# Conv 1: the scaling of the nodes' centred rows on ScalarE in eight pieces in place of one VectorE operation

## The reference, cut to what matters

```python
h = jnp.maximum(_layernorm(x, axis=-1), 0.0)
x = x + _L0_gnn_ref(h, edge_index, edge_attr_2, W1, root1, bias1, W2, root2, bias2)
# in it, twice (spline_conv):
xk = jnp.einsum('ni,kio->nko', x, W)              # 25 matrices of 64x64
msg = msg + basis[:, None] * xk[src, idx]         # four corners of the edge's cell
agg = jax.ops.segment_max(msg, dst, num_segments=N)
return agg + x @ root + bias                      # nodes without an edge: 0 + x @ root + bias
# the norm:
(x - m) / jnp.sqrt(v + eps)                       # m and v over the 64 channels of a node
```

## Time and profile before

| | |
|---|---|
| median of 3 runs | 1747.36 us |
| profiled execution | 1748.64 us, its span 1746.8 us |
| mean granted TensorE clock | 0.955 of full speed |
| busy over the span: PE | 1471.2 us, 84% |
| DVE (VectorE) | 1395.1 us, 80% |
| POOL (GpSimd) | 1225.4 us, 70% |
| ACT (ScalarE) | 731.8 us, 42% |

### The profile page before, as it was taken

The page is one execution under the profiler, slowest core; times in us unless marked ns, Lnnn a source line. Parts: engine busy times, 40 slices in busy tenths (PEclk is TensorE's granted clock), DMA queues, the critical chain, the costliest instruction groups (busy, mean ns, idle before and its releaser), DMA issues.

```text
span 1746.8 us, 33764 instructions
## 1 busy us (share of the span) xinstructions
PE 1471.2 (84%) x7834; PEld 1002.3 (57%) x7834; DVE 1395.1 (80%) x2704; ACT 731.8 (42%) x1840; POOL 1225.4 (70%) x1207
## 2 busy tenths in 40 slices
PE   3978888888888879999999999997777777777673
PEld 2856666666666656777777777774444333333332
DVE  6259999999999957988888888885776666666664
ACT  3533333333333353333333333335554555555553
POOL 5027777777777757777777777743677777777776
PEclk8989999999999979999999999997998999998998
DMA  8994444444445435878787777863333233323330
GB/s 136 160 121 107 105 106 110 105 107 107 110 104 108 98 91 155 213 215 216 213 212 209 208 209 211 208 177 82 78 70 70 69 70 70 72 71 66 73 72 18
DMA packets 451934, 218.45 MB, mean 125 GB/s; under 512 B 306089, under 2 KB 432058, under 8 KB 451896
## 3 DMA queue, kind: packets, MB, share of 16 engines
q1 hardware_dynamic: 355584, 138.37, 31.1%
q0 software_dynamic: 44864, 65.52, 17.6%
q10 hardware_dynamic: 51448, 14.14, 6.4%
HBM read 128.08 MB, written 92.64 MB: 126 GB/s over the span
## 4 chain that ended last, share of the span: by engine, by line
PE 34%; POOL 9%; issue 8%; ACT 5%; DVE 4%; DMA 4%; POOLq 0%; DVEq 0%; ACTq 0%; SPq 0%
PE bank L1016 17%; POOL gath L610 5%; POOL out_dram L617 4%; PE bank L1009 3%; PE bank L1146 3%; DMA gath<-M,gidx 2%; PE bank L1077 2%; PE bank L1060 2%; PE bank L1165 1%; DVE arena L1636 1%; PE bank L1049 1%; PE bank L1038 1%; PE bank L1069 1%; DVE arena L1624 1%; ACT arena L915 1%
## 5 line engine op out<-in xcount | busy, mean ns | idle before, releaser
L1016 PE MATMUL bank<-Wk,arena 128*128 128x320 f32 (+1 forms) x2352 | 652.8, 460 | 56.9 <-ACT arena L786 56.9
L610 POOL DMA_INDIRECT gath<-T,gidx x392 | 397.6, 1014 | 121.5 <-issue 117.6
L1016 PEld LDWEIGHTS bank<-Wk,arena 128*128 128x128 f32 (+1 forms) x2352 | 328.2, 189 | 262.0 <-issue 145.5
L786 ACT ACTIVATE arena<-bank 128x256 f32<-128x256 f32 (+1 forms) x392 | 169.7, 433 | 349.7 <-PE bank L1009 349.6
L610 POOL DMA_INDIRECT gath<-in_x_dram,gidx x196 | 194.7, 993 | 141.8 <-ACT gidx L706 83.3
L610 POOL DMA_INDIRECT gath<-M,gidx x196 | 211.1, 1077 | 108.6 <-issue 54.5
L617 POOL DMA_INDIRECT T<-srow,sidx x196 | 206.7, 1055 | 69.6 <-issue 59.4
L617 POOL DMA_INDIRECT out_dram<-srow,sidx x196 | 199.7, 1019 | 61.4 <-issue 60.8
L1425 DVE TENSOR_TENSOR arena<-bank,A 128x320 f32<-128x320 f32 x392 | 190.9, 487 | 57.7 <-PE bank L1016 53.6
L1009 PE MATMUL bank<-ident,arena 128*128 128x128 f32 x980 | 171.7, 274 | 12.4 <-DVE arena L1405 12.4
L1009 PEld LDWEIGHTS bank<-ident,arena 128*128 128x128 f32 x980 | 124.1, 141 | 43.4 <-issue 12.6
(11 more groups left out here) (212 smaller groups left out, 2685.9 us busy)
## 6 DMA issues: line engine op xcount, KB each, us to landing
T<-arena SPq DMA_DIRECT2D x96, 272.0 KB, 3.9
arena<-T SPq DMA_DIRECT2D x48, 544.0 KB, 5.5
T<-zero ACTq DMA_DIRECT2D x1, 13281.2 KB, 100.9
B<-arena SPq DMA_DIRECT2D x49, 256.0 KB, 3.3
arena<-B SPq DMA_DIRECT2D x49, 256.0 KB, 3.7
arena<-in_x_dram SPq DMA_DIRECT2D x48, 256.0 KB, 4.0
out_dram<-arena SPq DMA_DIRECT2D x48, 256.0 KB
begins_cut<-begins_d SPq DMA_DIRECT2D x49, 128.5 KB, 3.4
```

What stands on the lines that cost most here:

```text
L610: pool.indirect_dma_start(out=gath[slot][:, j, k, 0:width], out_offset=None, in_=table, in_offset=bass.IndirectOffsetOnAxis(gidx[slot][:, ...
L786: act.activation(ZT[j // 2][:, first:first + chunks, :], bank[j % 2][:, 0:chunks * P], ACT.Relu)\
L1016: return pe.matmul(bank[2 + r][:, 0:KO], ZT[q][rows, chunk, :], Wk[n - 1][rows, weights].rearrange("p k o -> p (k o)"), start=start, stop= ...
```

## The change

ScalarE does what `node_in` did: eight `activation` instructions with function Copy, one for each of the eight node tiles, each with its reciprocal deviation (one value per partition, a column of `jst`) as scale. They stand in ScalarE's step behind the index copy `gidx1(g + 3)` and ahead of the two small copies; the last of them signals `xn`. `node_in` leaves VectorE's step. As ScalarE now reads the reciprocals, VectorE's `roots` waits for `xn` of group e - 2 before it writes new ones.

```diff
+                    if n == 1 and g.within(G):
+                        wait(act, s["norm"], g + 1, "rstd")
+                        wait(act, s["ncen"], g)
+                        wait(act, s["npe"], g - 1, "nt")
+                        for t in range(NPP):
+                            scaled = act.activation(nh[:, t, :], nln[:, t, :], ACT.Copy,
+                                                    scale=jst[:, 3, TPG + t:TPG + t + 1])
+                        scaled.then_inc(s["xn"].sem, 1)
...
-                def node_in(g):
-                    wait(dve, s["norm"], g + 1, "rstd")
-                    wait(dve, s["npe"], g - 1, "nt")
-                    V_.tensor_tensor(nh[:, :, :], nln[:, :, :],
-                                     jy[:, TPG:].unsqueeze(2).broadcast_to([P, NPP, C]), ALU.mult)\
-                        .then_inc(s["xn"].sem, 1)
...
                     def roots():
                         if stats:
                             wait(dve, s["root"], e)
+                            wait(dve, s["xn"], e - 2)
                             V_.reciprocal(jy, jt).then_inc(s["norm"].sem, 1)
 
-                    if now and n == 1:
-                        node_in(g)
                     if ahead and n == 1:
                         scaled(g + 1)
```

## The result

The changed kernel takes 1751.67 us, the median of 13 runs (1748.94 to 1754.53); the kernel before took 1747.36 on the same chip (13 runs, 1744.55 to 1750.21). The ratio is 1.0025 [1.0016, 1.0033]: slower by 0.25%, or 4.3 us. The forecast was 12.6 us slower. The profiled span grew from 1746.8 to 1751.8 us.

A forecast was written before the change was run, and what follows sets the result against it. GpSimd was to bound conv 1 once VectorE got faster: 43 groups at 10.98 us gave +14.5, less 0.4 and 1.2, so +12.9 on the profiled 1748.64, 1761.5; 1.3 lower for the median gave 1760 us, range 1737 to 1782.

The forecast's parts named there:

- GpSimd is at work all the time and becomes the bound: Conv 1: GpSimd works or issues throughout its 10.52 us group; once VectorE is faster, GpSimd sets the pace.
- Its stalls come from VectorE's operations on two SBUF inputs: Conv 1: GpSimd's DMAs are held beside such VectorE operations; stalls of 0.40 us a group before the change.
- ScalarE's copies cost nothing: Conv 1, ScalarE: eight copies, 1.6 to 3.0 us a group, hidden in 3.67 us idle before its evacuation.
- The size of the stalls when VectorE follows GpSimd: Conv 1, GpSimd: 0.86 us a group, near attention's 0.77 and a little up, giving 10.98 us a group.
- the sum's 12.9: Whole kernel: +14.5 us over 43 conv 1 groups, -0.4 for the margin, -1.2 in the last two groups.
- The floor of 10.12: Conv 1, GpSimd: a group of four undisturbed gathers and four undisturbed scatters with gaps takes 10.12 us.
- rival 3: Conv 1: GpSimd has no stalls, 1723 us, or is no limit at all, 1718 us; chance 0.07.
- VectorE alone could go at 9.92: Conv 1, VectorE: removing L1452's 0.60 us shortens its loop from 10.52 to 9.92 us a group.
- The margin at the end: End of conv 1: time from the fourth gather's start to VectorE's use falls from 3.34 to about 2.9 us.
- Rival 1: Conv 1: GpSimd's stalls fall to 0.2 us a group with a lucky landing, 10.32 us, 1737 us; chance 0.12.
- rival 2: Conv 1: the phase locks again with about today's 0.40 us of stalls a group, 1746 us; chance 0.10.
- Rival 4: Conv 1: a DMA lands before a 1.9 us row of VectorE operations each group, stalls 1.4, 1784 us; chance 0.15.

The follow-up runs named there:

- e4_after_light: The changed kernel with three scatters a group in conv 1 in place of four; 1742.06 us, 0.9947 of the kernel before.
- e10_one_input: The changed kernel with nine VectorE operations in a conv 1 group written as reductions reading one SBUF input; 1735.14 us, 0.9924 of the kernel before.
- e1_both: The changed kernel with a spare VectorE product on two SBUF inputs in the removed operation's place, copies kept; 1752.92 us, 1.0000 of the kernel before.
- e3_one_copy: The changed kernel with one unscaled ScalarE copy of 128x512 in place of the eight; 1763.3 us, 1.0056 of the kernel before.
- e11_pad_small: The changed kernel with a 128-column fill of a spare tile on VectorE ahead of the normalisation's sums; 1740.64 us, 0.9952 of the kernel before.
- e12_pad_large: The changed kernel with a 240-column fill of a spare tile on VectorE ahead of the normalisation's sums; 1746.29 us, 0.9989 of the kernel before.
- e2_reduce: The changed kernel with a spare VectorE reduction on one SBUF input in the removed operation's place; 1752.1 us, 0.9997 of the kernel before.
- e6_before_evac: The kernel before with ScalarE's fourth evacuation of the group moved ahead of its squares; 1760.56 us, 1.0064 of the kernel before.
- e7_before_order: The kernel before with VectorE's node bias addition moved between the first and second message additions; 1759.23 us, 1.0049 of the kernel before.

## Why the prediction was right or wrong, point by point

**GpSimd is at work all the time and becomes the bound: right.** VectorE waits for the gathered rows in 34 groups of this stretch; with a scatter fewer (e4_after_light) or with its stalls taken away (e10_one_input) the wait is gone and the change is a gain.

**Its stalls come from VectorE's operations on two SBUF inputs: right,** by e10_one_input. The prediction weighed the Trainium skill here, SBUF — State Buffer, "Who interferes with whom", which infers that descriptor generation is not held up by such an operation. For these indirect DMAs, which take their row indices from a tile in SBUF, e10_one_input shows that the issuing instruction is held up (means of 1.018 and 1.063 us with the operations, 0.961 and 0.998 without), and the measurement decides. Whether it is held in reading the indices, which the same section's rule for GpSimd instructions that read SBUF would cover, or in making descriptors, no run here tells.

**ScalarE's copies cost nothing: right,** by e1_both, where the loss is gone with the copies in place, and e3_one_copy, where seven of them are gone and the loss is not. They took 2.00 us and not 1.6, inside the bounds given; 1.76 us of cover were left.

**The size of the stalls when VectorE follows GpSimd: this is the step that failed.** Taken were 0.86 us a group, so 10.98; measured were 10.78 - 10.12 = 0.66 over the 43 groups and 0.64 in the settled part. Over 43 groups that is 43 x 0.20 = 8.6 us, more than the whole distance between the sum's 12.9 and the 5.0 measured. The value came from attention's stalls, 0.77, and a little up. Attention runs other operations, and a stall is set by what VectorE runs beside the DMAs, as e10_one_input showed; that attention's stalls could be taken over had no other ground than the same eight DMAs. The bounds of zero and 1.70 were too wide to correct it. If VectorE waits for the fourth gather, the places of the DMAs against its operations follow from the landing, so the loop could have been walked in the trace of before. I did not do that, and with two patterns in the changed kernel it is not shown that it would have given 0.66.

The floor of 10.12 was too low as well. It takes the shortest gather and scatter for all four; the undisturbed group is 10.27, by e10_one_input. So the 0.40 read as stalls of the kernel before were 0.25, nearly all of them L1452's, and of the 0.66 only 0.51 are stalls (0.46 in the settled part). The sum adds floor and stalls, so this moved no time in the forecast by itself, but rival 3's 1723 rests on it.

**VectorE alone could go at 9.92: wrong.** Ahead of the first wait most groups took 10.24 to 10.26, and with room on GpSimd (e4_after_light) the mean is 10.27. I had found one loop over other engines, and it held L1452. There is another over TensorE, from L1510 to the first weighing and back to L1510, which doesn't: in the changed kernel VectorE waits 0.3 to 0.4 us ahead of L1433 (307.48 above). Of the 0.60 us removed only 0.23 to 0.25 were to be had. In this kernel it changed little, for GpSimd bounds it anyway with its 10.27 and its stalls; rival 3's 1718 was never within reach.

**The small terms.** The margin at the end is 2.54 us (606.06 to 608.60) rather than 2.9. But the sum counts from the first gather of the last group, not from the fourth, and from there to the use the time fell from 7.15 to 6.70, near the forecast 0.4. Behind it conv 1's tail gave 0.4 us rather than 1.2. Not in the sum were the later start, 0.65, and the 0.8 that the later stages give back; nothing here says where they come from.

**The rivals.** Rival 1 (10.32 with lucky stalls) and rival 2 (the phase locks again) did not happen in the changed kernel, but both exist: e11_pad_small is about the first, e12_pad_large and e2_reduce the second. "Nothing pulls GpSimd back into step" was right for VectorE's 10.27; the 10.34 of e11_pad_small is enough to do it. Rival 4's 1.4 us of stalls is excluded by the 0.66. The times of rivals 1 and 2 are reckoned from 10.52 a group and those of 3 and 4 from the 10.64 with the drift; from 10.64 the first two would have been about 5 us less.

**Open.** Why e3_one_copy and e6_before_evac lose more (10.84 and 10.87) than the changed kernel; the trace gives no order in which the two engines were granted what they compete for; what starts the single knocks of e7_before_order.

## What to carry to other kernels

Where two engines have the same period and one has no wait but "issue", the stalls of that one fill its free time: its floor decides what a faster partner is worth, and a partner sped up past it can make the whole slower. Then take the work off the engine that lies at its floor, or take away what stalls it; and when that can't be done, try the faster engine a little slower, at the pace that the other can just follow (10.34 instead of 10.27 us a group made it 0.48% faster than the kernel before). Take an engine's floor from an undisturbed group and not from its shortest instruction: here that gives 10.27 and not 10.12, and the other engine's loop is 10.27 as well. To size such a regime, try to walk its loop in the trace, from the late landing through the operation that delays the next DMA, rather than borrow the stalls of another stage, and look at more than two groups: the loop can have more than one pattern.

## What the runs showed of the hardware

GpSimd's indirect DMA of 128 rows takes 0.94 to 1.02 us undisturbed with 0.30 us between two of them (e10_one_input: four gathers 0.99, 0.97, 0.94, 0.94, four scatters 1.02, 1.00, 0.98, 0.98), and one was drawn out to 2.25 beside VectorE (298.73 in e7_before_order). I had expected its excess to be a fixed property of a group; it depends on what VectorE runs and on the phase between the two: none with nine operations on one input in place of two, 0.46 us a group in the changed kernel, 0.25 in the kernel before. A ScalarE copy of 128x64 with a scale per partition lasts 0.335 us, yet the next starts 0.24 us after it.
